# A layer of sparse attention and routed experts on one core: the first routed tile moved between the last shared down products, the last tile's activation cut in pieces, GpSimd's index copies ahead of their wait

## The reference

```python
x = x + attn(layernorm(x))          # 32 heads of 8, 8 key/value heads; keys j with i-128 <= j < i are masked out
h = layernorm(x)                    # 2048 rows
scores = sigmoid(h @ w_router.T)    # 8 experts
topk_w, topk_i = top_k(scores, 2); topk_w /= topk_w.sum(-1)
out = sum over the two of topk_w * (silu(h @ wg[e].T) * (h @ wu[e].T)) @ wd[e].T      # inner width 640
out += sum over 2 shared experts of (silu(h @ sg.T) * (h @ su.T)) @ sd.T
x = x + out
```

## Time and profile before

| | us |
|---|---|
| median of 3 runs (lowest, highest) | 905.71 (905.21, 905.88) |
| the profiled execution's own time | 906.11 |
| its span, first to last instruction | 904.4 |
| PE busy in the span | 870.5 (96%) |
| ACT, DVE, POOL busy | 578.6, 450.7, 276.2 |

### The profile page before, as it was taken

How to read it: one execution, slowest core, us unless ns; L and a number is a source line. 1 busy time by engine, 2 the same in 40 slices (tenths; PEclk the granted TensorE clock), 3 DMA queues, 4 the chain that set the end, 5 groups by cost and what they waited for, 6 DMA issues and landing times.

```text
span 904.4 us, 22574 instructions
## 1 busy us (share of the span) xinstructions
PE 870.5 (96%) x8167; PEld 561.6 (62%) x8168; DVE 450.7 (50%) x776; ACT 578.6 (64%) x733; POOL 276.2 (31%) x423
## 2 busy tenths in 40 slices
PE   8989999999999999999999999999999999999994
PEld 5524444433434343343447888888888989999983
DVE  8644443344444334454548677667834343434332
ACT  4789999999999999999993433342222222222220
POOL 5043334333333433333340000000024454544442
PEclk9979999999999999999999999999999999999998
DMA  6345444665544466733102206100037875575421
GB/s 189 122 132 185 151 164 164 218 214 210 193 154 162 161 219 228 244 99 90 31 13 76 70 27 240 50 1 24 1 101 217 269 226 160 158 205 154 121 36 23
DMA packets 42062, 124.43 MB, mean 138 GB/s; under 512 B 7668, under 2 KB 23028, under 8 KB 35824
## 3 DMA queue, kind: packets, MB, share of 16 engines
q1 hardware_dynamic: 31152, 110.35, 35.9%
q0 software_dynamic: 7072, 9.72, 6.0%
q10 hardware_dynamic: 3744, 3.02, 1.0%
HBM read 74.03 MB, written 49.02 MB: 136 GB/s over the span
## 4 chain that ended last, share of the span: by engine, by line
PE 79%; ACT 13%; issue 4%; DVE 2%; DMA 1%; POOL 0%; ACTq 0%; POOLq 0%; DVEq 0%
PE ps L1737 18%; PE ps L1910 14%; PE ps L1690 13%; PE ps L1864 12%; ACT arena L958 12%; PE ps L1932 7%; PE ps L1877 6%; PE ps L1921 2%; PE ps L1631 2%; PE ps L1791 2%; PE ps L1891 1%; DMA out<-arena,now_to 0%; PE ps L1821 0%; DMA xres<-x 0%; PE ps L1851 0%
## 5 line engine op out<-in xcount | busy, mean ns | idle before, releaser
L958 ACT ACTIVATE arena<-ps 128x1024 f32<-128x1024 f32 x336 | 319.9, 1063 | 2.0 <-PE ps L1690 2.0
L1737 PE MATMUL ps<-arena 128*32 128x256 f32 x4096 | 265.6, 386 | 0.6 <-POOL arena L785 0.6
L785 POOL TENSOR_SCALAR_AFFINE_SELECT arena<-arena 128x512 f32<-128x512 f32 x240 | 150.1, 638 | 265.7 <-ACT arena L969 258.0
L1690 PE MATMUL ps<-arena 64*128 64x512 bf16 (+1 forms) x1280 | 176.9, 343 | 12.1 <-ACT arena L958 8.5
L1737 PEld LDWEIGHTS ps<-arena 128*32 128x32 f32 x4096 | 112.4, 110 | 99.1 <-issue 42.4
L1690 PEld LDWEIGHTS ps<-arena 64*128 64x128 bf16 x1280 | 57.7, 94 | 157.9 <-ACT arena L958 79.5
L1189 DVE COPY_PREDICATED ps<-keep,ps 128x512 f32<-128x512 int32 (+1 forms) x128 | 80.6, 629 | 143.8 <-PE ps L1690 143.8
L1910 PE MATMUL ps<-wr_all,x2T 128*128 x648 | 141.3, 362 | 2.0 <-issue 1.0
L1910 PEld LDWEIGHTS ps<-wr_all,x2T 128*128 128x128 f32 x648 | 106.7, 189 | 19.5 <-issue 4.1
L1864 PE MATMUL ps<-x2T,wr_all 128*128 128x512 f32 x480 | 116.8, 394 | 1.3 <-issue 1.2
L969 ACT ACTIVATE arena<-ps 128x1024 f32<-128x1024 f32 x112 | 112.4, 1062 | 0.5 <-PE ps L1690 0.4
(11 more groups left out here) (198 smaller groups left out, 706.1 us busy)
## 6 DMA issues: line engine op xcount, KB each, us to landing
w_scr<-wr_all SPq DMA_DIRECT2D x24, 1280.0 KB, 7.3
wr_all<-w_scr SPq DMA_DIRECT2D x24, 1280.0 KB, 6.1
raw<-w_experts SPq DMA_DIRECT2D x24, 640.0 KB, 7.8
arena<-q_scr SPq DMA_DIRECT2D x64, 64.0 KB
o_scr<-arena SPq DMA_DIRECT2D x128, 32.0 KB, 1.7
arena<-o_scr SPq DMA_DIRECT2D x16, 256.0 KB, 4.0
raw<-w_shared SPq DMA_DIRECT2D x6, 640.0 KB, 5.0
q_scr<-parts SPq DMA_DIRECT2D x8, 384.0 KB, 3.0
```

The costliest lines, as they stand in the source:

```text
L785: nc.gpsimd.affine_select(out=dst, in_=src, compare_op=ALU.is_ge if own else ALU.is_gt, fill=0.0, base=0, pattern=[[0, REP], [-1 if own el ...
L958: nc.scalar.activation(prob[:, SLOT[unit(a, kt)], :, :].rearrange("p h q -> p (h q)"), score.rearrange("p b x -> p (b x)"), ACT.Exp, scale ...
L1690: return nc.tensor.matmul(ps[:, bank, :].rearrange("p (h q) -> p h q", h=2)[:, :, place * P:(place + tiles) * P], kst[r0:r0 + HALF, s, kt ...
L1737: last = nc.tensor.matmul(ps[32 * h:32 * h + 32, 6 + qc, a % 2 * QW:(a % 2 + 1) * QW], vst[:, s, kt, :], prob[:, SLOT[k], h, :], start=(no ...
```

## The change

- Into the shared stage: for chunk 0, ACT copies the first bank alone, and DVE copies the second.
- Shared to routed: on PE the up products of tile 0 and the transposes of tile 1 go between the downs of steps 38 and 39, behind a wait for the last `s_hid`. ACT's copy and DVE's rest for tile 0's rows go into step 39, ahead of `s_hi` and `s_split` of that step. DVE does `xT_low(1)` and `up(0)` before it waits for the last down. Tile 0's inner rows are turned into banks 3 and 6, so that only tile 1's transposes wait for `s_out`; ACT and DVE take them out in two instructions each. `gact[0]` and `hid[0]` get memory of their own.
- Last tile: `e_gu` goes up after each of its last two pieces, so the Silu starts after the first of them; DVE's product is cut at column 384, and the second part waits for the last piece; the transposes and the copies go by `LAST_PARTS`.
- POOL: `add` waits for `e_y` last, after the copy, the register read and the wait for earlier adds.
- The loops of ACT, DVE and POOL are written out as PE's is.

```diff
         top[0] = HSH
-        gact = carve(2 * I).rearrange("p (s i) -> p s i", s=2)
-        hid = carve(2 * I).rearrange("p (s i) -> p s i", s=2)
+        gact, hid = ([None, carve(I)] for _ in range(2))
         ysb = carve(2 * D).rearrange("p (s d) -> p s d", s=2)
+        top[0] = HSH + HR * 2 * CT + 2 * 2 * CT
+        gact[0], hid[0] = carve(I), carve(I)
...
-                pool.wait_ge(e_y, j + 1 + FIRST)
                 stage(now_to[:, p:p + 1], slot_to[:, ds(j, 1)], n)
...
                 wait_apart(pool, e_added[1 - p], after)
+                wait_apart(pool, e_y, j + 1 + FIRST)
                 nc.gpsimd.indirect_dma_start(
...
-            pairs = for_pairs(pool, 2, pair_rows)
+            pairs = for_pairs(pool, 2, pair_rows, True)
             for j in range(4):
...
                 act.wait_ge(c_tp, c + 1)
-                for k in range(KD):
+                for k in range(KD if c else 1):
                     nc.scalar.copy(x2T[:, 0, k, ds(c * CT, CT)], ps[:, XT_BANK[c] + k, :]).then_inc(c_xT, 1)
...
                     nc.scalar.activation(gsh[:, q % 2, :], ps[:, 2 * (q % 2), :], ACT.Silu).then_inc(s_act, 1)
+                    if step == NC * STEPS - 1:
+                        xT_out(0, 0)
                     act.wait_ge(s_hid, step + 1 + FIRST)
...
+            def xT_out(j, p):
+                act.wait_ge(e_tx, j + 1)
+                nc.scalar.copy(xsT[:, p, 0], ps[:, 7, 0:D].rearrange("p (k t) -> p k t", k=KD)).then_inc(e_xT, 1)
+
+            def hT_out(j, p):
+                act.wait_ge(e_th, j + 1)
+                if isinstance(j, int) and j == 0:
+                    nc.scalar.copy(hidT[:, 0, 0, 0:4].rearrange("p k t -> p (k t)"), ps[:, 3, :])
+                    nc.scalar.copy(hidT[:, 0, 0, 4], ps[:, 6, 0:P]).then_inc(e_hThi, 1)
+                    return
+                nc.scalar.copy(hidT[:, p, 0].rearrange("p k t -> p (k t)"),
+                               ps[:, 4:6, :].rearrange("p b n -> p (b n)")[:, 0:I]).then_inc(e_hThi, 1)
+
+            def gate(j, p):
+                act.wait_ge(e_gu, j + 1)
+                nc.scalar.activation(gact[p][:, :], ps[:, 0:3, :].rearrange("p b n -> p (b n)")[:, 0:I], ACT.Silu) \
+                    .then_inc(e_act, 1)
+
             root(NC + 1)
...
                 shared(c)
-
-            def xT_out(j, p):
-                act.wait_ge(e_tx, j + 1)
-                nc.scalar.copy(xsT[:, p, 0], ps[:, 7, 0:D].rearrange("p (k t) -> p k t", k=KD)).then_inc(e_xT, 1)
-
-            def hT_out(j, p):
-                act.wait_ge(e_th, j + 1)
-                nc.scalar.copy(hidT[:, p, 0].rearrange("p k t -> p (k t)"),
-                               ps[:, 4:6, :].rearrange("p b n -> p (b n)")[:, 0:I]).then_inc(e_hThi, 1)
-
-            def gate(j, p):
-                act.wait_ge(e_gu, j + 1)
-                nc.scalar.activation(gact[:, p, :], ps[:, 0:3, :].rearrange("p b n -> p (b n)")[:, 0:I], ACT.Silu) \
-                    .then_inc(e_act, 1)
-
-            xT_out(0, 0)
             xT_out(1, 1)
...
             act.wait_ge(r_tiles, 5)
-            j = for_pairs(act, 1, pair) * 2 + 2
+            j = for_pairs(act, 1, pair, True) * 2 + 2
             hT_out(j, 0)
             gate(j + 1, 1)
-            act.wait_ge(e_th, j + 2)
             for i, (k0, k1) in enumerate(LAST_PARTS):
+                act.wait_ge(e_th, j + (2 + i))
                 nc.scalar.copy(hidT[:, 1, 0, k0:k1].rearrange("p k t -> p (k t)"), ps[:, 4 + i, 0:(k1 - k0) * P]) \
...
                 dve.wait_ge(c_tp, c + 1)
+                if c == 0:
+                    nc.vector.tensor_copy(x2T[:, 0, 1, 0:CT], ps[:, XT_BANK[c] + 1, :]).then_inc(c_xT, 1)
                 dve.wait_ge(c_xT, c * KD + KD)
...
                     between(step)
+                    if step == NC * STEPS - 1:
+                        xT_low(0, 0)
                     dve.wait_ge(s_hi, step + 1)
...
                 if c == NC - 1:
-                    xT_low(0, 0)
+                    xT_low(1, 1)
+                    up(0, 0)
                 dve.wait_ge(s_down, c + 1)
...
                 dve.wait_ge(e_act, j + 1)
-                nc.vector.tensor_tensor(hid[:, p, :], gact[:, p, :],
+                nc.vector.tensor_tensor(hid[p][:, :], gact[p][:, :],
                                         ps[:, 0:3, :].rearrange("p b n -> p (b n)")[:, I:2 * I], ALU.mult) \
...
                 dve.wait_ge(e_hThi, j + 1)
+                if isinstance(j, int) and j == 0:
+                    nc.vector.tensor_tensor(hidT[:, 0, 1, 0:4].rearrange("p k t -> p (k t)"), ps[:, 3, :],
+                                            hidT[:, 0, 0, 0:4].rearrange("p k t -> p (k t)").bitcast(F32), ALU.subtract)
+                    nc.vector.tensor_tensor(hidT[:, 0, 1, 4], ps[:, 6, 0:P], hidT[:, 0, 0, 4].bitcast(F32), ALU.subtract) \
+                        .then_inc(e_hT, 1)
+                    return
                 nc.vector.tensor_tensor(hidT[:, p, 1].rearrange("p k t -> p (k t)"),
...
                 shared(c, routing)
-
-            xT_low(1, 1)
-            up(0, 0)
...
-            j = for_pairs(dve, 1, routed_pair) * 2 + 2
+            j = for_pairs(dve, 1, routed_pair, True) * 2 + 2
             hT_low(j, 0)
-            up(j + 1, 1)
+            dve.wait_ge(e_act, j + 2)
+            n = 1024 - I
+            nc.vector.tensor_tensor(hid[1][:, 0:n], gact[1][:, 0:n], ps[:, 1, I - 512:512], ALU.mult)
+            dve.wait_ge(e_gu, j + 3)
+            nc.vector.tensor_tensor(hid[1][:, n:I], gact[1][:, n:I], ps[:, 2, 0:I - n], ALU.mult).then_inc(e_hid, 1)
             y_out(j, 0)
...
                     last = nc.tensor.transpose(ps[:, bank, column * P:(column + 1) * P],
-                                               hid[:, p, k * P:(k + 1) * P], ident[:, :])
+                                               hid[p][:, k * P:(k + 1) * P], ident[:, :])
                 last.then_inc(e_th, 1)
...
                 pe.wait_ge(e_y, j + FIRST)
-                starts = {k0: i for i, (k0, _) in enumerate(parts)}
-                for k in range(KI):
-                    if k in starts:
-                        pe.wait_ge(e_hT, j + (starts[k] + 1 + FIRST))
+                for i, part in enumerate(parts):
+                    pe.wait_ge(e_hT, j + (i + 1 + FIRST))
+                    last = down_rows(p, slot, range(*part))
+                last.then_inc(e_mm, 1)
+
+            def down_rows(p, slot, rows):
+                for k in rows:
                     for w, v in PRODUCTS:
...
                                                 stop=(k == KI - 1 and (w, v) == PRODUCTS[-1]))
-                last.then_inc(e_mm, 1)
+                return last
...
-                routed_hT(j, p)
+                if isinstance(j, int) and j == 0:
+                    routed_hT(0, 0, lambda k: (3, k) if k < 4 else (6, 0))
+                elif isinstance(j, int) and j == 1:
+                    pe.wait_ge(s_out, NC * TPC + FIRST)
+                    routed_hT(1, 1)
+                else:
+                    routed_hT(j, p)
                 slot_next = slot_next()
...
                 shared_down(c, STEPS - 2)
+                if c == NC - 1:
+                    slot = slot_tile(0)
+                    pe.wait_ge(s_hid, NC * STEPS + FIRST)
+                    routed_up_first(0, 0, slot, later=False)
+                    routed_xT(1, 1, 0)
+                    routed_up(0, slot, PIECES[1:]).then_inc(e_gu, 1)
                 shared_down(c, STEPS - 1)
-                if c == NC - 1:
-                    routed_xT(1, 1, 0)
...
                 shared(c)
-            slot = slot_tile(0)
-            routed_up_first(0, 0, slot, later=False)
-            routed_up(0, slot, PIECES[1:]).then_inc(e_gu, 1)
             routed_up_first(1, 1, slot_tile(1))
...
-            pe.wait_ge(s_out, NC * TPC + FIRST)
             j = for_pairs(pe, 1, pair_of_tiles, True) * 2 + 2
-            slot_1, slot_0 = routed_rest(j, 0, lambda: slot_tile(j + 1), None, lambda: slot_tile(j))
-            routed_down(j, 0, slot_0)
-            routed_hT(j + 1, 1, lambda k: (4, k) if k < LAST_PARTS[1][0] else (5, k - LAST_PARTS[1][0]))
+            routed_hT(j, 0)
+            slot_1 = slot_tile(j + 1)
+            routed_up(1, slot_1, PIECES[1:2]).then_inc(e_gu, 1)
+            slot_0 = slot_tile(j)
+            routed_up(1, slot_1, PIECES[2:]).then_inc(e_gu, 1)
+            pe.wait_ge(e_y, j + FIRST)
+            pe.wait_ge(e_hT, j + (1 + FIRST))
+            down_rows(0, slot_0, range(KI)).then_inc(e_mm, 1)
+            pe.wait_ge(e_hid, j + 2 + FIRST)
+            for i, (k0, k1) in enumerate(LAST_PARTS):
+                for k in range(k0, k1):
+                    last = nc.tensor.transpose(ps[:, 4 + i, (k - k0) * P:(k - k0 + 1) * P], hid[1][:, k * P:(k + 1) * P],
+                                               ident[:, :])
+                last.then_inc(e_th, 1)
             routed_down(j + 1, 1, slot_1, LAST_PARTS)
...
```

(4 more changed lines are left out.)

4 lines of the change are left out of this document (added).

## The result

| | before | changed |
|---|---|---|
| median of 11 runs each (lowest, highest), us | 905.71 (904.75, 905.92) | 903.24 (902.48, 903.62) |
| span of the profiled execution | 904.4 | 901.7 |
| PE busy | 870.5 | 869.3 |

The account below looks back on a forecast made before the run. PE was taken as full in the routed loop, with time to win only at three places outside it. Terms 0.38 + 0.98 + 0.25 + 1.05 = 2.66 us off 905.71 gave some 903.0, range for 8 in 10 902.0 to 904.3.

Parts of the forecast that it names:

- Into the shared stage: Start of the shared stage: DVE makes the second copy beside ACT's first, 0.38 us won, bounds 0.3 and 0.45.
- Between the stages: Shared to routed: PE's stall before tile 1's first piece goes, 0.98 us won, bounds 0.5 and 1.15.
- Written-out loops: Routed loop: ACT, DVE and POOL lose loop overhead, but PE is full there, so nothing won.
- POOL's slower rival: Routed loop: written-out POOL sets the pace and tiles take longer, 909.5 us at 0.3 a tile; chance 0.05.
- The last tile and POOL's order: End of kernel: last down 0.25 us earlier, and 1.05 us less from the last y_out to the last add.
- The sum: Whole kernel: all terms together, 2.66 us won, median some 903.0 us.
- The rival in which the add's start is the DMA instruction's own: POOL's adds: most of the 1.5 us before each belongs to the DMA, new order wins 0.2; chance 0.15.
- The rival in which the stall only moves: Between the stages: PE waits for tile 0's rest, the Silu or the two-piece rest, 0.98 us lost; chance 0.08.

Follow-up runs that it names:

- the rolled kernel: Changed kernel with the loops of ACT, DVE and POOL rolled again from the second pair on; median 903.27 us, ratio 0.9969 to the kernel before.
- the one-piece run: Changed kernel with the last tile's activation, product and transposes in one piece each, the copies still in two; median 903.41 us.
- wait_32: Changed kernel with the last four adds staged ahead, the last add's wait number worked out as 288 (tile 32's add landed); median 902.95 us.
- wait_34: Changed kernel with the last four adds staged ahead, the last add's wait number worked out as 304 (tile 34's add landed); median 904.65 us.
- pe_fewer_reads: Changed kernel, but PE doesn't reread tile 0's and 1's slots in the first pair and reads the number of pairs after the second; median 903.04 us.
- last_add_free: Changed kernel with the last four adds staged ahead and the very last add not waiting for earlier adds; median 902.97 us.

## Why the prediction was right

**Into the shared stage**: forecast 0.38, measured 0.37, and 0.38 by the run that undoes it. DVE's price, taken from its pieces' rows, was 0.69 as measured.

**Between the stages**: the stall went as worked out, and a little more than its 0.98 with it (1.11). The term came out at 0.80 and not at 1.21 because of what I gave as the reason for the lower bound, a register read on PE behind the last down; I put no number on it, and 0.41 was given back. It is one read that took 0.91 us and not 0.30. The number of reads alone would not have done it: the kernel before has them too, with a gap of 0.17. That `s_out` and with it SP's row store come later was foreseen (675.4, measured 674.6), but not that a read would fall on the store's start. Expert 1's load began 2.94 later (675.14 against 672.20; 3.3 to 3.7 forecast), but the fourth block, expert 2's first, was issued at 694.32 and not at 697.5 as that would give, and tile 7's gather did not wait for its weights. The two-instruction copies for tile 0 were covered: DVE's rest, 0.69 from 675.91 and 0.28 behind it, is over by 676.8, 1.2 before the down. The cut cost 0.69 + 0.28 - 0.82 = 0.15, the 157 ns of the prediction, and as the Trainium skill ("VectorE: DVE Perf Modes", section "The TRN2 errata") has it, once for each further instruction.

**Written-out loops**: nothing in the runs, as forecast. POOL's slower rival is refuted: the way to tile 34's down is no longer for it. What the forecast does not have is the step of 0.33 in POOL's tail, which the rolled kernel lacks.

**The last tile and POOL's order**: forecast 0.25 + 1.05 = 1.30, measured 1.02. The 0.80 to 0.82 from `y_out` to an add whose staging is done is what I took from the gathers with register numbers (0.81). Two things were off. The pieces won more on PE than I gave them, and more than my upper bound of 0.35 (0.46, of which the one-piece run gives 0.38 to them), and nothing at the end. And the step that failed is "POOL is free at about 893.0, and 0.18 + 1.51 less the final wait of 0.81 brings it to 893.9, before 894.24": POOL is not ready before the last `y_out`. That step gives POOL about 2.4 us from the start of tile 34's add (1.05 before 892.49) to the last wait; it took 3.10. The copy was done after 1.77, nearly as I had it, but the register read and the waits took 1.33 and not 0.70: 0.33 is the step in POOL's instructions, and in the rolled kernel, which lacks it, they still took 0.99. In six of the kernels with the new order and the old staging the last add therefore stands 3.86 or 3.87 behind tile 34's, and 3.53 in the rolled one.

Before the change the chain ran through the last `y_out` (1.86 behind it); now it runs through tile 34's `y_out` and POOL. The spacing of the two adds is nearly what it was (3.86, now 3.87), so the whole tail won what tile 34's add won, 1.84 - 0.80 = 1.04. That the two spacings are equal is chance, for they have different reasons. The prediction has this 1.05 beside its sum, for another reason, a landing that binds; wait_32 and wait_34 exclude that reason.

**The sum**: 2.66 forecast, 2.47 measured between the medians, and 2.29 when the distances are added up. Part of the closeness is luck: the first two terms together came out 0.19 low and the tail 0.28 low, and inside the tail two errors of opposite sign partly cancel (0.46 for 0.25 on PE, 0.56 for 1.05 on POOL, each read at the last add).

The rival in which the add's start is the DMA instruction's own is refuted by the 0.80. The rival in which the stall only moves came true by less than half (0.41 of 0.98), by a slow register read and not by the waits it names.

## What to carry to other kernels

When a chain at the end goes through a slow in-order engine, count that engine's whole distance from one of its steps to the next, and not only what it does after the last input: here 0.38 us won on TensorE were worth nothing because GpSimd needed 3.87 from add to add. A reordering also moves other engines' transfers: here the row store came to start where TensorE reads a register, and that read took three times as long. Where the order of use is known, keep such values in registers; it gave 0.81 us. And a number that makes a wait look like the cause is settled by keeping the instructions and changing the number, not by taking the wait out. Even then, look in the sequencer's records before putting a price on the instructions: taking some out also shifts all that follow them.

## What the runs showed of the hardware

- A register read on PE took 0.30 us, and 0.88 to 0.91 in the nine kernels in which it began 0.06 to 0.13 us after the first packet of the row store. PE hides four reads of usual length in a pair of tiles (12.1 us) and shows the fifth as 0.36 us (pe_fewer_reads, tile 5).
- In all twelve traces with POOL's loop written out a step of about 0.33 us stands at one place in POOL's tail; in the kernel before and the rolled one it doesn't. It costs 0.33 when it falls between `y_out` and the add (1.14 against 0.81 in wait_32 and last_add_free).
- Waiting for a landed add cost 1.27 from landing to the next start, that step of about 0.33 included (wait_34).
- The releaser beside the last add (a landed add, in rows 5 and in the changed kernel) was not its cause; wait_32 and wait_34 show that.
- The start of the shared stage differs by over 1 us between executions behind unchanged code, more than several of the effects here; the distances inside a stage don't.
